# Spectral and convolution stages of a graph-network kernel: groups worked four at a time, one rectification moved to GpSimd

## The reference

```python
h = jnp.maximum(_layernorm(x, axis=-1), 0.0)
# layer 0 (spectral), U from eigh of the normalised Laplacian
agg = jnp.einsum('mn,bnd->bmd', U.T, features)
h = jax.nn.relu(agg @ W1 + b1)
out = h @ W2 + b2
x = x + jnp.einsum('nm,bmd->bnd', U, out)
# layer 2 (convolution twice, then LSTMs over windows of 1 to 4)
h = jax.nn.relu(jnp.einsum('ts,bsh->bth', adj, x @ Wg0 + bg0))
h = jax.nn.relu(jnp.einsum('ts,bsh->bth', adj, h @ Wg1 + bg1))
```

## Time and profile before

| | |
|---|---|
| runs | 1392.74, 1395.27, 1395.79 us, median 1395.27 |
| profiled execution, its span | 1392.23 us, 1390.5 us |
| TensorE matmul busy | 1008.1 us (73%) |
| VectorE, ScalarE, GpSimd busy | 983.2, 725.7, 354.1 us |
| chain that ended last, by engine | PE 56%, DVE 27%, issue 8%, ACT 5%, POOL 2% |

### The profile page before, as it was taken

How to read it: one execution, slowest core, us unless ns; L and a number is a source line. 1 busy time by engine, 2 the same in 40 slices (tenths; PEclk the granted TensorE clock), 3 DMA queues, 4 the chain that set the end, 5 groups by cost and what they waited for, 6 DMA issues and landing times.

```text
span 1390.5 us, 21788 instructions
## 1 busy us (share of the span) xinstructions
PE 1008.1 (73%) x5403; PEld 632.4 (45%) x5403; DVE 983.2 (71%) x3979; ACT 725.7 (52%) x2037; POOL 354.1 (25%) x1155
## 2 busy tenths in 40 slices
PE   3666666666534234068887778899999999689997
PEld 1444444445522123045553466444466544456665
DVE  8777888888888998965687844344455655677786
ACT  1333444444425243534566567686566544477775
POOL 4035555666625666000100010001022410100000
PEclk9999999999999998569999789999999999799999
DMA  5000000000020000000000000000000000000011
GB/s 155 1 0 1 1 1 1 1 2 1 2 55 1 0 1 1 1 1 0 0 0 0 0 1 0 0 0 0 0 1 0 0 0 1 1 16 23 23 30 32
DMA packets 16662, 12.37 MB, mean 9 GB/s; under 512 B 666, under 2 KB 14531, under 8 KB 16579
## 3 DMA queue, kind: packets, MB, share of 16 engines
q1 hardware_dynamic: 16578, 11.49, 3.0%
HBM read 7.23 MB, written 4.19 MB: 8 GB/s over the span
## 4 chain that ended last, share of the span: by engine, by line
PE 56%; DVE 27%; issue 8%; ACT 5%; POOL 2%; DMA 1%; DVEq 1%; ACTq 0%; POOLq 0%
PE P L1459 30%; PE P L714 13%; DVE arena L369 2%; DVE arena L489 2%; PE P L1608 2%; DVE bst_all L934 2%; ACT hb L1243 2%; DVE arena L494 1%; DVE arena L487 1%; DVE bcol L388 1%; PE P L1601 1%; PE P L1614 1%; PE P L1579 1%; PE P L1597 1%; DVE scal L357 1%
## 5 line engine op out<-in xcount | busy, mean ns | idle before, releaser
L1459 PE MATMUL P<-arena,WT 128*128 128x336 f32 (+2 forms) x792 | 302.2, 542 | 4.1 <-ACT L1346 2.9
L1459 PEld LDWEIGHTS P<-arena,WT 128*128 128x128 f32 x792 | 149.7, 190 | 150.9 <-issue 119.1
L714 PE MATMUL P<-arena 1*128 1x127 f32 (+62 forms) x504 | 150.8, 428 | 89.3 <-DVE arena L369 87.1
L1354 ACT ACTIVATE arena<-P,bl 128x512 f32<-128x512 f32 (+1 forms) x252 | 152.4, 635 | 61.2 <-PE P L1459 55.2
L714 PEld LDWEIGHTS P<-arena 1*128 1x128 f32 x504 | 122.1, 308 | 131.3 <-DVE arena L366 120.5
L653 ACT ACTIVATE arena<-arena 1x127 f32<-1x127 f32 (+62 forms) x126 | 32.3, 256 | 165.8 <-DVE arena L380 155.5
L923 POOL COPY arena<-arena 128x336 f32<-128x336 f32 (+1 forms) x40 | 43.4, 1096 | 267.3 <-PE P L1459 146.7
L1243 ACT ACTIVATE hb<-xN,nmr,rsd 128x128 f32 (+1 forms) x192 | 78.4, 481 | 42.5 <-PE P L1459 30.6
L201 POOL TENSOR_SCALAR lf<-lf 1x1 f32<-1x1 f32 x210 | 86.8, 413 | 21.9
L714 PE MATMUL P<-arena,Ib 128*128 128x46 bf16 (+1 forms) x318 | 35.5, 273 | 64.0 <-ACT arena L683 63.4
L714 PE MATMUL P<-I,bcol 128*1 128x128 f32 (+62 forms) x252 | 47.8, 287 | 35.5 <-DVE bcol L388 35.5
(11 more groups left out here) (500 smaller groups left out, 2532.5 us busy)
## 6 DMA issues: line engine op xcount, KB each, us to landing
out_dram<-xN SPq DMA_DIRECT2D x16, 256.0 KB, 2.3
Wn<-in_L_gnn_Wih_dram SPq DMA_DIRECT2D x4, 256.0 KB, 2.7
Wn<-in_L_gnn_Whh_dram SPq DMA_DIRECT2D x4, 256.0 KB, 2.6
Wqkv<-in_L_gnn_W_dram SPq DMA_DIRECT2D x1, 192.0 KB
W1n<-in_L_gnn_W_dram SPq DMA_DIRECT2D x1, 128.0 KB
W2n<-in_L_gnn_W_dram SPq DMA_DIRECT2D x1, 128.0 KB
Wg<-in_L_gnn_Wg_dram SPq DMA_DIRECT2D x2, 64.0 KB
adj<-in_adj_dram SPq DMA_DIRECT2D x1, 64.0 KB, 1.8
```

The source lines that it names most:

```text
L714: def mm(o,l,r,start=True,stop=True): return t.matmul(o,lhsT=l,rhs=r,start=start,stop=stop)
L1354: act(s.gt[u][gate][:,0:cols],P[4*u+gate][:,0:cols],f,bias=s.bl[:,4*(p-1)+gate:4*(p-1)+gate+1]).then_inc(ev('lstm_gates'),1)
L1459: def mm(o,l,r,start=True,stop=True,**k): return t.matmul(o,lhsT=l,rhs=r,start=start,stop=stop,**k)
```

## The change

Both stages run over NQ = 4 quads of four groups, unrolled, without a loop. Each of a group's four products is issued for four groups in a row. The quad has all eight banks: the first and the third product of group g use P[g%4], the second and the fourth P[4+g%4]. Every buffer gets two more slots, in `R1`. ScalarE makes three of the next quad's `h` ahead of its rectifications and the fourth behind them. VectorE alternates the next quad's copies with this quad's statistics. In the convolution the last rectification goes from ScalarE to GpSimd (`gpsimd_gcn`), whose queue has it between the scales of layer 3 and the LSTM's windows; the copy for its first turn is no longer ahead of the last residual statistics. TensorE gets waits for the last residual sums. The core of the diff; the removed bodies stand in the listing above, and the new lines of ScalarE and TensorE for the convolution follow the pattern of the spectral ones:

```diff
--- before.py
+++ after.py
+        net.gpsimd_gcn(eng)
...
+    s.spectral_hb,s.spectral_zb,s.spectral_rb=(t+[slot(25+2*k+u) for u in range(2)] for k,t in enumerate((s.hb,s.zb,s.rb)))
+    s.spectral_ob=s.ob+[slot(31),slot(15)]
+    s.conv_hb,s.conv_zb,s.conv_yb=(t+[slot(25+2*k+u) for u in range(2)] for k,t in enumerate((s.hb,s.zb,s.yb)))
+    s.conv_rb,s.conv_ob,s.conv_cb=(t+[slot(2*k+u) for u in range(2)] for k,t in enumerate((s.rb,s.ob,s.cb)))
...
+  def gpsimd_gcn(s,eng):
+
+    for g in range(NG):
+        eng.wait_ge(s.ev('conv_out'),g+3)
+        eng.tensor_scalar(s.R2[:,g*C:(g+1)*C],s.conv_cb[g%4][:,:],0.0,None,ALU.max).then_inc(s.ev('conv_gcn'),1)
...
-    def residual_a(it,more):
...
+    def spectral_copy(g):
+        v.wait_ge(ev('spectral_product1'),g+1)
+        v.tensor_copy(s.spectral_zb[g%4][:,:],P[g%4][:,:]).then_inc(ev('spectral_mixed'),1)
+    def spectral_stats(g):
+        v.wait_ge(ev('spectral_x'),g+3)
+        s.ln_stats(v,xN,g)
+    for g in range(4): spectral_copy(g)
+    for it in range(NQ):
+        quad=range(4*it,4*it+4)
+        for g in quad:
+            v.wait_ge(ev('spectral_product3'),g+1)
+            tt(g4(s.spectral_ob[g%4][:,:]),g4(P[g%4][:,:]),b4(s.b2bc),ALU.add).then_inc(ev('spectral_out'),1)
+        if it==NQ-1: s.layer_inverse(v,2,0)
+        for g in quad:
+            v.wait_ge(ev('spectral_product4'),g+1)
+            tt(X(g),X(g),P[4+g%4][:,:],ALU.add).then_inc(ev('spectral_x'),1)
+        if it==NQ-1: copy_z('expand_',0)
+        for g in quad:
+            if it<NQ-1: spectral_copy(g+4)
+            spectral_stats(g)
...
     for u in range(2): residual(0,NP-1,u)
-    copy_z('conv_',0)
     for u in range(2): residual_stats(0,NP-1,u)
...
+    for it in range(NQ):
+        quad=range(4*it,4*it+4)
+        for g in quad:
+            v.wait_ge(ev('conv_product1'),g+1)
+            v.tensor_copy(s.conv_zb[g%4][:,:],P[g%4][:,:]).then_inc(ev('conv_mixed'),1)
+        for g in quad:
+            v.wait_ge(ev('conv_product2'),g+1)
+            tt(g4(s.conv_yb[g%4][:,:]),g4(P[4+g%4][:,:]),b4(s.bg0t),ALU.add).then_inc(ev('conv_y'),1)
+        if it==0: s.layer_inverse(v,3,1)
+        for g in quad:
+            v.wait_ge(ev('conv_product4'),g+1)
+            if it: v.wait_ge(ev('conv_gcn'),g-3)
+            tt(g4(s.conv_cb[g%4][:,:]),g4(P[4+g%4][:,:]),b4(s.bg1t),ALU.add).then_inc(ev('conv_out'),1)
...
-    def relu_a(it,more):
...
+    def spectral_h(g):
+        if g>=4: a.wait_ge(ev('spectral_product1'),g-3)
+        for b in range(GB):
+            i=act(s.spectral_hb[g%4][:,b*N:(b+1)*N],s.xN[:,g*C+b*N:g*C+(b+1)*N],ACT.Relu,bias=s.nmr[:,g*GB+b:g*GB+b+1],scale=s.rsd[:,g*GB+b:g*GB+b+1])
+        i.then_inc(ev('spectral_h'),1)
+    for g in range(4): spectral_h(g)
     a.wait_ge(ev('biases'),1)
-    with a.Fori(0,NP-1) as it: relu_a(it,True)
-    relu_a(NP-1,False)
+    for it in range(NQ):
+        if it<NQ-1:
+            for u in range(3): spectral_h(4*it+4+u)
+        for g in range(4*it,4*it+4):
+            a.wait_ge(ev('spectral_product2'),g+1)
+            act(s.spectral_rb[g%4][:,:],P[4+g%4][:,:],ACT.Relu,bias=s.bcol('L0_gnn_b1')).then_inc(ev('spectral_relu'),1)
+        if it<NQ-1: spectral_h(4*it+7)
...
-            act(R2[:,bass.ds(g*C,C)],s.cb[u][:,:],ACT.Relu).then_inc(ev('conv_gcn'),1)
...
+    for g in range(4): conv_h(g)
     s.layer_roots(a,3,1)
-    with a.Fori(1,5) as it: layer_e(it,True)
-    s.last_scales(a,3)
-    with a.Fori(5,NP-1) as it: layer_e(it,True)
-    layer_e(NP-1,False)
+    for it in range(NQ):
+        quad=range(4*it,4*it+4)
+        if it==NQ-2: s.last_scales(a,3)
+        if it<NQ-1:
+            for u in range(3): conv_h(4*it+4+u)
+        for g in quad:
+            a.wait_ge(ev('conv_y'),g+1)
+            act(s.conv_rb[g%4][:,:],s.conv_yb[g%4][:,:],ACT.Relu).then_inc(ev('conv_relu'),1)
+        for g in quad:
+            a.wait_ge(ev('conv_product3'),g+1)
+            act(s.conv_ob[g%4][:,:],P[g%4][:,:],ACT.Copy).then_inc(ev('conv_copied'),1)
+        if it<NQ-1: conv_h(4*it+7)
     a.preload_act_table(ACT.Sigmoid)
...
+    for it in range(NQ):
+        quad=range(4*it,4*it+4)
+        for g in quad:
+            t.wait_ge(ev('spectral_h'),g+1)
+            mix(P[g%4],s.spectral_hb[g%4],s.U[:,:]).then_inc(ev('spectral_product1'),1)
+        for g in quad:
+            t.wait_ge(ev('spectral_mixed'),g+1)
+            if it: t.wait_ge(ev('spectral_x'),g-1)
+            mm(P[4+g%4][:,:],s.W0a[:,:],s.spectral_zb[g%4][:,:]).then_inc(ev('spectral_product2'),1)
+        for g in quad:
+            t.wait_ge(ev('spectral_relu'),g+1)
+            mix(P[g%4],s.spectral_rb[g%4],s.W0b[:,:]).then_inc(ev('spectral_product3'),1)
+        for g in quad:
+            t.wait_ge(ev('spectral_out'),g+1)
+            mm(P[4+g%4][:,:],s.UT[:,:],s.spectral_ob[g%4][:,:]).then_inc(ev('spectral_product4'),1)
+    t.wait_ge(ev('spectral_x'),NG)
...
+        for g in quad:
+            t.wait_ge(ev('conv_mixed'),g+1)
+            if it: t.wait_ge(ev('conv_out'),g-1)
+            else: t.wait_ge(ev('residual_x'),NG+2)
+            mix(P[4+g%4],s.conv_zb[g%4],s.Wg0[:,:]).then_inc(ev('conv_product2'),1)
...
+        for g in quad:
+            t.wait_ge(ev('conv_copied'),g+1)
+            mm(P[4+g%4][:,:],s.Wg1[:,:],s.conv_ob[g%4][:,:]).then_inc(ev('conv_product4'),1)
```

More of the change, by code:

```diff
@@ L823 @@
 NP=NG//2
+NQ=NG//4
 FIRST_GROUPS=12
@@ L1281, in ahead @@
             s.act_ln(a,it+1,stage,(u,))
-    def relu_a(it,more):
[L1283 to L1287, removed]
-    a.wait_ge(ev('biases'),1)
-    with a.Fori(0,NP-1) as it: relu_a(it,True)
-    relu_a(NP-1,False)
+    def spectral_h(g):
[4 more added lines that the diff above has]
+    for g in range(4): spectral_h(g)
+    a.wait_ge(ev('biases'),1)
+    for it in range(NQ):
[5 more added lines that the diff above has]
+        if it<NQ-1: spectral_h(4*it+7)
     a.sem_inc(ev('expand_hidden_first'),2)
@@ L1326, in scalar_main, with conv_h @@
     s.first_scales(a,3)
[L1327 to L1337, removed]
-            act(R2[:,bass.ds(g*C,C)],s.cb[u][:,:],ACT.Relu).then_inc(ev('conv_gcn'),1)
-    s.act_ln(a,0,'conv_')
-    layer_e(0,True)
-    s.layer_roots(a,3,1)
-    with a.Fori(1,5) as it: layer_e(it,True)
-    s.last_scales(a,3)
-    with a.Fori(5,NP-1) as it: layer_e(it,True)
-    layer_e(NP-1,False)
+    def conv_h(g):
+        if g>=4: a.wait_ge(ev('conv_product1'),g-3)
+        for b in range(GB):
+            i=act(s.conv_hb[g%4][:,b*N:(b+1)*N],s.xN[:,g*C+b*N:g*C+(b+1)*N],ACT.Relu,bias=s.nmr[:,g*GB+b:g*GB+b+1],scale=s.rsd[:,g*GB+b:g*GB+b+1])
+        i.then_inc(ev('conv_h'),1)
+    for g in range(4): conv_h(g)
+    s.layer_roots(a,3,1)
+    for it in range(NQ):
[10 more added lines that the diff above has]
+        if it<NQ-1: conv_h(4*it+7)
     a.preload_act_table(ACT.Sigmoid)
@@ L1503, in tensor @@
             i.then_inc(ev('residual_product'),1)
[L1504 to L1517, removed]
+    for it in range(NQ):
+        quad=range(4*it,4*it+4)
+        for g in quad:
+            t.wait_ge(ev('conv_h'),g+1)
+            mix(P[g%4],s.conv_hb[g%4],s.adjT[:,:]).then_inc(ev('conv_product1'),1)
+        for g in quad:
[3 more added lines that the diff above has]
+            mix(P[4+g%4],s.conv_zb[g%4],s.Wg0[:,:]).then_inc(ev('conv_product2'),1)
+        for g in quad:
+            t.wait_ge(ev('conv_relu'),g+1)
+            mix(P[g%4],s.conv_rb[g%4],s.adjT[:,:]).then_inc(ev('conv_product3'),1)
+        for g in quad:
+            t.wait_ge(ev('conv_copied'),g+1)
+            mm(P[4+g%4][:,:],s.Wg1[:,:],s.conv_ob[g%4][:,:]).then_inc(ev('conv_product4'),1)
     t.wait_ge(ev('conv_gcn'),NG)
```

## The result

| | before | changed |
|---|---|---|
| runs, median | 1394.01 us (1391.34 to 1395.79, 4 runs) | 1362.48 us (1361.97 to 1363.38, 4 runs) |
| profiled execution, its span | 1392.23, 1390.5 us | 1361.97, 1360.2 us |

The account below looks back on a forecast made before the run. TensorE's products were taken to wait for other engines' copies, with two groups too few to fill the time; 13.4 + 15.4 + 1.1 = 29.9 us off 1392.23 gives 1362.3, plus 3.0 to the median, 1365.4; range 1360.5 to 1374.

Parts of the forecast that it names:

- What bounds the kernel: Both stages: TensorE's products wait for copies; pairs take 18.7 and 18.6 us per four groups, against 14.4 and 14.56 without waits.
- The pace of a quad: Four groups without stalls at 0.92 us per `mix` and 0.88 per 512 columns: 14.4 us spectral, 14.56 convolution.
- The margins: Spectral quad: VectorE's fourth copy ready at 6.1, wanted at 6.3; ScalarE's first rectification ready at 6.5, wanted at 7.2.
- Spectral stage: First expand `h` at 670.4 instead of 685.44, 15.0 us earlier; first expand product at 672.1 instead of 687.14.
- Expand joint: Eight more statistics behind the expand copies on VectorE's queue cost 1.6 us, or 0 with slack; 13.4 are left.
- Convolution: Convolution stage: the last bias add starts at 865.5 instead of 880.93, 15.4 us gained.
- The end: Joint to the LSTM: table load hidden, GpSimd's rectification taken as 0.9 us; 1.1 us gained.
- VectorE held up by GpSimd: Rival, chance 0.07: the last three bias adds each wait for a GpSimd rectification of 0.9, end 2.7 later, 1368.1.
- The clock: Rival, chance 0.10: clock falls before the expand stage, costing 1.6 us, 1367.0; or holds before the LSTM, 1363.8.
- The other half of that rival: Clock rival's lucky side: gap before the LSTM shrinks to about 1.9 us, clock holds, 1.6 won, 1363.8.
- half of the gain: Rival, chance 0.08: results 0.5 us later stall VectorE's copy each quad, 3 to 8 us less gain, 1368 to 1373.
- the slower case: Rival, chance 0.02: TensorE at half clock for a whole stage, 55 us lost, 25 slower than before, 1420.

Follow-up runs that it names:

- statistics first: Changed kernel with VectorE's statistics ahead of the copy of each group within each spectral quad instead of behind it: 1365.25 us, ratio 0.98.
- the last quad on ScalarE: Changed kernel with the convolution's last four rectifications on ScalarE behind the sigmoid table load, the other twelve on GpSimd: 1358.51 us, ratio 0.975.
- The two experiments that split the joint: Changed kernel with two groups' statistics ahead of the expand copies, 1362.13 us; changed kernel with only VectorE's signal for `W1T` ahead of them, 1362.15 us.
- both joints with the early signal: Changed kernel with two groups' statistics and the `W1T` signal ahead of the expand copies, and the last quad's rectifications on ScalarE: 1356.79 us, ratio 0.9738.

## Why the prediction was right, and where it was off

**What bounds the kernel**: right that the pairs ran below TensorE's pace because products waited, and that four in a row end this; each stage alone gives its half. The reason given for the waits is only in part right. A product, its small operation and their signals take about 1.9 us (1.2 and 0.7), and two groups cover 1.72 to 1.79. That shortage is small, but for the convolution's rectification, which comes behind a bias add: from `Wg,zb` to its `adjT,rb` it is 2.60 us. The largest stall of each turn, 0.95 and 0.90, came from an `h` ahead of the rectification in ScalarE's queue, and the 0.48 came behind four statistics ahead of VectorE's copy; the prediction listed the latter's rows and did not read them so.

**The pace of a quad**: right in kind, a little slow in size. The terms 0.92 for a `mix` and 0.88 for 512 columns measured 0.893 and 0.86. Both had been taken from other places: a pair of `mix` in the loop over pairs, and the expand stage's products, which still take 0.88 in the changed kernel (675.49 to 678.99 for four). So 14.4 and 14.56 were 14.01 and 14.16 us, some 0.4 too much for each of three full quads a stage: 1.2 us a stage.

**The margins**: VectorE's fourth copy, forecast at 6.1 against 6.3, ended 5.89 us after its quad's start against 6.15, and one group's statistics later, 0.8 us, it stalled for 0.38 (statistics first). ScalarE's chain held, even with the rectifications that the change takes away from it.

**Spectral stage**: forecast 15.0 us, the stretch shrank by 16.97; 1.2 of the difference of 2.0 is the quads' pace, the rest lies in the first quad. The reciprocal followed the fourth bias add at once, and the first `h` came 2.31 us after it, as taken from the earlier trace rows. In that quad 0.5 us is luck with the clock: it was full 3.1 us after the first product, and 4.1 after it in the kernel before, so a microsecond less ran at half speed. In the version with the last quad on ScalarE it was still 0.65 over 617 to 619, and in the one with groups of four in the spectral stage only it was full after 6.0 us; this stretch ranges from 58.9 to 60.4 over the traces.

**Expand joint**: forecast 1.6 given back, measured 1.49. The two experiments that split the joint show that it is the statistics on VectorE's queue. The wait for the signal behind them was not foreseen, and cost nothing.

**Convolution**: forecast 15.4, measured 16.78; the quads' pace is nearly all of the difference.

**The end: the mis-sized term.** The prediction took g = 0.9 for GpSimd's rectification, midway between 0.29 and 1.49, and so a gain of 1.1. It measured 1.484, the upper bound, with all four in a queue, and the joint grew by 1.73: 2.8 us off, with the other sign. The prediction's own formula for 1.49, 2.4 less, comes within 0.4. The row of equal size, 512 columns, had it within 10 ns; the row of equal kind, 0.29 for 128 columns, would give 1.17 for four times as many, so the middle of the two was too low by either. The Trainium skill, "GPSIMD Engine Reference" (section 3), gives 769 ns as its best case for 512 elements; the measurement is nearly twice that, and decides. Its warning against GpSimd for ordinary elementwise arithmetic is borne out, at the end of a stage rather than by a rate inside: ScalarE does the same rectification in 0.63 us.

The two errors, 3.35 us too little in the two stages and 2.8 too much at the end, nearly cancel: the sum of 29.9 us gave 1362.3 for the profiled execution, and that took 1361.97. That it comes so close is luck. The median lies 2.9 under its forecast for another reason: the step that put 3.0 us between profiled execution and median, which was so for the three runs of before, and is 0.5 for the changed kernel. That step was the weakest, with three runs behind it; with the fourth run of before it is 1.8.

**The rivals.** VectorE held up by GpSimd: its last adds took 0.69 with GpSimd at work beside them, as with ScalarE in its place, so this costs nothing here. By the Trainium skill, "SBUF — State Buffer" (on its two sides), GpSimd holds up VectorE only in a two-port mode or with two inputs from SBUF. The trace agrees: these adds read one operand from SBUF and one from PSUM. The clock: it fell in the expand joint in two of the ten traces with spectral quads (statistics first, and both joints with the early signal), where the joint was 1.7 and 1.3 us longer for it, and in neither of the changed kernel's two. The other half of that rival needed a gap of about 1.9 us before the LSTM. The gap was 4.59, and the clock fell; with the last quad on ScalarE it was 1.92, the clock held, and 1.45 us came, near the 1.6 that the prediction gave. The prediction read that TensorE restarted the LSTM at half speed in the kernel before; in fact the first 1.1 us ran at full speed, and the 3.4 us at half behind them cost 1.7, about what it said. No stalls inside the quads, and both stages of the changed kernel ran at full clock but for their first 3.1 and 5.3 us, so neither half of the gain nor the slower case came.

## What to carry to other kernels

When each product waits for a small operation on another engine, count how many independent groups in a row cover that round trip, and look at what else stands ahead of the small operation in its engine's queue: here four groups took 18.7 us as two pairs and 14.0 in one row, and the largest stall of the pairs came from such a queue. Then look at what the regrouping leaves at the ends of the stage: whatever is done for four groups at once also queues up four times where the next stage waits, and there the fastest engine should do it. Moving work off an engine that has slack gained nothing here.
